# Moving accumulations and masking products on the vector engine inside a state-space loop

## The reference

```python
proj = hidden @ in_proj_w.T
gate, xBC, dt = split(proj)                  # gate and x: 8192 channels, B and C: 8 groups of 128
xBC = silu(causal_conv4(xBC))
scores = einsum(C, B) * exp(segment sums)    # Lmat, lower triangle, chunks of 128 positions
Ydiag = scores @ (x * dt)                    # within a chunk
Yoff  = C @ (carried state) * exp(cs)        # from the chunk before
y = (Ydiag + Yoff + x * D) * silu(gate)
out = y * rsqrt(mean(y*y over a group)) * norm_w @ out_proj_w.T
```

## Time and profile before

| | us |
|---|---|
| median of 3 runs | 2202.49 |
| lowest and highest | 2200.89, 2202.69 |
| the profiled execution | 2201.61 |
| span of its trace | 2199.8 |
| PE busy | 2129.0 (97%) |
| DVE busy | 1642.6 (75%) |
| ACT busy | 1431.4 (65%) |
| POOL busy | 1038.7 (47%) |

### The profile page before, as it was taken

The page is one execution under the profiler, slowest core; times in us unless marked ns, Lnnn a source line. Parts: engine busy times, 40 slices in busy tenths (PEclk is TensorE's granted clock), DMA queues, the critical chain, the costliest instruction groups (busy, mean ns, idle before and its releaser), DMA issues.

```text
span 2199.8 us, 34805 instructions
## 1 busy us (share of the span) xinstructions
PE 2129.0 (97%) x12594; PEld 1744.9 (79%) x12604; DVE 1642.6 (75%) x2661; ACT 1431.4 (65%) x3090; POOL 1038.7 (47%) x755
## 2 busy tenths in 40 slices
PE   7989989999899999999999999999999999999999
PEld 7866687887788878888888887887887888777887
DVE  7777673234888898888898888889889888886221
ACT  4388734334977677668767867767867777773332
POOL 5477544352255346344455434534445443553442
PEclk9999999999999999999999999999999999999999
DMA  3000012331423232233223323323322332231332
GB/s 134 1 1 2 1 44 83 95 92 48 168 96 135 87 125 97 87 135 126 95 87 125 130 75 113 118 78 121 135 87 87 134 135 87 87 114 49 91 96 82
DMA packets 65337, 202.53 MB, mean 92 GB/s; under 512 B 7056, under 2 KB 9104, under 8 KB 56976
## 3 DMA queue, kind: packets, MB, share of 16 engines
q1 hardware_dynamic: 65168, 200.31, 27.0%
HBM read 197.39 MB, written 2.88 MB: 91 GB/s over the span
## 4 chain that ended last, share of the span: by engine, by line
PE 83%; ACT 7%; DVE 6%; issue 3%; DMA 0%; POOL 0%; DVEq 0%; ACTq 0%; SPq 0%; POOLq 0%
PE ps L1683 78%; ACT eb L899 2%; PE ps L1987 2%; PE ps L1805 2%; PE ps L1698 1%; DVE PT L1305 1%; ACT eb L906 1%; DVE nm L1283 1%; ACT yTh L913 1%; ACT work L862 0%; DVE eb L1432 0%; ACT wAh L691 0%; ACT xc L878 0%; ACT pr_a L772 0%; DVE bst L1125 0%
## 5 line engine op out<-in xcount | busy, mean ns | idle before, releaser
L551 POOL TENSOR_TENSOR wAl<-rawA,wAh 128x512 fp32r<-128x512 f32 x233 | 339.6, 1470 | 382.5 <-ACT wAh L691 381.7
L1683 PE MATMUL ps<-xTh,wAh 128*128 128x512 f32 x1512 | 424.5, 402 | 5.7 <-DVE oacc L1500 2.6
L1683 PE MATMUL ps<-xTh,wAl 128*128 128x512 f32 x1512 | 414.7, 395 | 0.0
L1683 PE MATMUL ps<-xTl,wAh 128*128 128x512 f32 x1512 | 414.6, 395 | 0.0
L1393 DVE SCALAR_TENSOR_TENSOR work<-ps,chp,work 128x510 f32<-128x510 f32 (+2 forms) x465 | 343.9, 743 | 32.1 <-ACT work L862 22.1
L1683 PEld LDWEIGHTS ps<-xTh,wAl 128*128 128x128 f32 x1512 | 284.2, 188 | 69.4
L1683 PEld LDWEIGHTS ps<-xTl,wAh 128*128 128x128 f32 x1512 | 284.0, 188 | 69.3
L1683 PEld LDWEIGHTS ps<-xTh,wAh 128*128 128x128 f32 x1512 | 275.5, 188 | 74.9 <-issue 14.3
L557 POOL TENSOR_TENSOR wBl<-rawB,wBh 128x512 fp32r<-128x512 f32 x108 | 138.4, 1295 | 392.1 <-ACT wBh L695 392.1
L899 ACT ACTIVATE eb<-eb,gc 128x128 f32<-128x128 f32 x1008 | 307.6, 391 | 0.0
L862 ACT ACTIVATE work<-ps,gpar 128x512 f32<-128x512 f32 x155 | 119.4, 770 | 154.4 <-PE ps L1683 121.9
(11 more groups left out here) (208 smaller groups left out, 3976.7 us busy)
## 6 DMA issues: line engine op xcount, KB each, us to landing
eb<-scr_decays SPq DMA_DIRECT2D x62, 1536.0 KB, 6.5
rawA<-ma_in SPq DMA_DIRECT2D x144, 256.0 KB, 6.8
rawA<-fa_in SPq DMA_DIRECT2D x88, 256.0 KB, 2.6
rawB<-mb_in SPq DMA_DIRECT2D x64, 256.0 KB, 2.8
rawB<-fb_in SPq DMA_DIRECT2D x44, 256.0 KB, 2.6
x<-x_in SPq DMA_DIRECT2D x8, 256.0 KB, 6.0
x_out<-x SPq DMA_DIRECT2D x8, 256.0 KB, 2.7
wqraw<-wqkv_in SPq DMA_DIRECT2D x1, 1536.0 KB, 10.8
```

Of the source, the lines that this page charges most:

```text
L551: nc.gpsimd.tensor_tensor(wAl[:, slot, :], rawA[:, slot, :], wAh[:, slot, :].bitcast(F32), ALU.subtract).then_inc(A_lo, 1)
L1683: return nc.tensor.matmul(o, l, r, start=start, stop=end, **kw)
```

## The change

In odd steps the evacuation of sum 0 moves from behind both `scale_x` to between them. In steps with v = 1 and g > 0 (seven of them) both `decay_off` move from the front of the sequence to behind the evacuations, directly ahead of `decay`. Nothing else moves, and no instruction is added or taken away.

```diff
             vn = next_step(v, g)
-            if not ending and not (first and v == 0):
+            late_off = (first and v == 0) or (v == 1 and g > 0)
+            if not ending and not late_off:
                 decay_off(*vn, 0)
                 decay_off(*vn, 1)
             if not ending:
                 scale_x(*vn, 0)
+            if v % 2 == 1:
+                evacuate(v, g, 0)
+            if not ending:
                 scale_x(*vn, 1)
             if v % 2 == 1:
-                for t in range(4):
+                for t in range(1, 4):
                     evacuate(v, g, t)
-            if first and v == 0:
+            if not ending and late_off:
                 decay_off(*vn, 0)
                 decay_off(*vn, 1)
```

## The result

| | us |
|---|---|
| after, median of 6 runs | 2186.65 (2185.47 to 2188.23) |
| before, median of 6 runs | 2202.24 (2200.89 to 2202.69) |
| ratio | 0.9931, 95% interval 0.9921 to 0.9941 |
| profiled execution after | 2186.76 |
| its span | 2184.9, before 2199.8 |

The change makes the kernel 0.7% faster.

The account below looks back on a forecast made before the run. PE was taken as the bound, busy 97% of the span. Per group, -1.88 us at sum 3 became +0.4 through POOL turns, +2.8 over seven; other terms zero. Forecast median 2205.3 us, range 2188 to 2209.

Parts of the forecast that it names:

- Copy of sum 0, and `decay_off` out of its way: Step v = 1, g > 0: PE's wait ahead of sum 3 goes, -1.88 us a group, bound 13.2 in all.
- What is late next: Late `decay_off` and `decay` alternate with POOL's squares; PE waits 2.18 us for sum 7: +0.4 a group, +2.8 in all.
- the first rival: DVE has the first turn against `sqt`, or one turn is skipped: -4.4 us, 2198.1 us; chance 0.18.
- Who has the first turn: `sqt`, issued 0.13 us ahead of `decay_off`, holds the ports first by the skill page's rule; otherwise 2198.1 us.
- DVE keeps its turn over instructions in a row: Rival: only the first `decay_off` waits for `sqt`, all of the 13.2 us gain stays, 2189.3 us; chance 0.16.
- Copy of sum 0 in the first group: Step v = 1 of g = 0: no updates ahead of the copies and no wait listed, so zero.
- The additions of sum 0 in steps 3, 5 and 7: They come 0.93 us earlier, PE did not wait; the second `scale_x`, 0.60 later, is hidden by DVE's wait: zero.
- everything else: Later DVE copies in v = 2, readers of `decay_off`, and SP's and ACT's waits: no further cost or gain.

Follow-up runs that it names:

- e1: Changed kernel with both `decay_off` put back at the front, copy of sum 0 still between the two `scale_x`; measured 2194.55 us, ratio 0.9967.
- e2: Changed kernel with all evacuations behind both `scale_x` again, `decay_off` still late; measured 2204.27 us, ratio 1.0012.
- e3: Changed kernel, DVE also waits for the end of its own copy 3 ahead of the first `decay_off`; measured 2211.06 us, ratio 1.0042.
- e10: Changed kernel with two added waits: DVE for its first `update`, POOL for its own `lo_B` ahead of the squares; measured 2197.41 us (one run).
- e5: Changed kernel, DVE also waits for the end of its own copy 0 in the seven steps; measured 2210.34 us (one run).
- e8: Changed kernel with DVE's wait for its own copy 3, POOL's four squares left out in the seven steps; measured 2186.49 us, ratio 0.9928.
- e7: Changed kernel, DVE also waits for the end of its first `update` in the seven steps; measured 2211.30 us (one run).

## Why the prediction was wrong

- *Copy of sum 0, and `decay_off` out of its way*: right. The bound was 1.88 a group and 13.2 in all; measured 1.92 and 13.5. e1 and e2 show that both edits are needed for it.
- *What is late next*: this is the step that failed, in its sentence "They take turns, one instruction each" and in "Now the four POOL instructions meet four of DVE". They did not take turns. `sqt` took 4.49 in place of 1.04, both `decay_off` 1.29 in place of the 3.1 to 788.11, and the second `decay` ended at some 788.7 in place of 792.31. The +2.8 is −13.5 in truth. I had taken the turns for a fixed trait of `sqt` and `sq` meeting DVE. Two things that the sum leaned on went otherwise, the lead and the stop.
- *The lead*: `sqt` at 784.89 against `decay_off` at 785.02 is 0.13, and 0.01 to 0.04 was measured. The sum let copy 3 start 1.70 behind sum 3, as before, but 0.10 of that belonged to PE's slow start, which goes away with the wait; from the first `update` to `decay_off` it is 6.23 and not the 6.30 of the sum. With a lead of 0.13 the turns come as forecast (e3), and at 0.12 without any recent stop (e1); so a tenth of a microsecond lay between the forecast and the result.
- *The stop*: with DVE first, turns were still possible, as in e10 and in the first rival; that they did not come goes with the distance from DVE's last stop; why it does stays open. In the rows with turns that I read for this place, DVE had stood still shortly before: copy 3 for 0.55 in the earlier trace rows, the addition for 0.63 in the earlier trace rows, and the `yTl` directly ahead of the `decay_off` at 804.95 for 0.69. The change takes away that very stand-still, because PE brings sum 3 earlier: copy 3 starts without one, at 784.61, some 0.06 after it could have had sum 3 (an estimate: 782.95 and the 1.60 that is left of 1.70). The prediction's own sum has this stand-still shrink from 0.55 to 0.05 (784.37 to 784.42) and does not remark on it. e1 loses it as well and keeps its turns, because there `sq` is 0.12 ahead: taking away the stand-still was not enough by itself. The question "whom does the edit make stop waiting" was asked for PE and not for DVE.
- The arithmetic of turns was right where turns happen: e3 has 14.3 us of waits where "about 15" was forecast, and +0.41 a group where +0.4 was, in the three groups in which the clock holds; e10 has 7.1 and 2197.41 where the first rival, with one turn less, said 2198.1.
- *Who has the first turn*: the Trainium skill's page "SBUF — State Buffer", section "Who interferes with whom", has whoever issues first hold the ports for the whole instruction. Here `sqt` was issued first, by 0.01 to 0.04, in seven of seven groups, and did not get them. The measurement decides. At leads of 0.12 and more (e1, e3, e5 to e8) the page's rule and the traces agree on the first turn.
- *DVE keeps its turn over instructions in a row*, the rival at 2189.3, is what happened. I gave it 0.16, though its row, `lo_A` with 3.43, was the only one of a DVE that had not just stopped: DVE's last stop ahead of the first `decay` there is one of 0.03 us at 757.94, 9.4 us back, and the `decay` is the 15th instruction behind it; the last longer one, 1.30 us for PE, ends at 755.78. It too was a little off: its sum lets the first `decay_off` wait for `sqt`, and in fact not even that one waits. Its wait would have been hidden, so the time is not touched by it.
- *Copy of sum 0 in the first group*: taken as zero, measured 0.39. PE, before, in g = 0:

```profile
602.28 0.61 PE L1683 MATMUL ps<-wBh,yTl 128*128 128x512 f32 x2
603.00 0.73 PE L1683 MATMUL ps<-wBh,yTh 128*128 128x512 f32 x2
```

After:

```profile
602.92 0.62 PE L1687 MATMUL ps<-wBh,yTl 128*128 128x512 f32 x2
603.37 0.62 PE L1687 MATMUL ps<-wBh,yTh 128*128 128x512 f32 x2
```

The distance is 0.72 before and 0.45 after: sum 3 was 0.27 late in group 0 too, with a slower start of 0.11 behind it. The list of waits does not have so short a one, and I took its silence for a zero.

- *The additions of sum 0 in steps 3, 5 and 7*, and *everything else*: zero was right, to 0.03 us a place.
- The 1.4 at the end and the 0.61 ahead of the loop are none of the change's; without them the span would be 14.1 shorter.

## What to carry to other kernels

When a change takes a wait away, follow it on every engine: another engine may stop waiting too, and here that moved a vector instruction by a tenth of a microsecond against one of POOL's and turned an alternation into a lock-out. Before rows of a meeting of two engines are carried to a new place, look at two things, and take rows that are alike in both: which instruction is issued first and by how much, and how long before it the vector engine last stopped. If the margin is of the order of 0.1 us, the forecast has two outcomes and should carry both. A semaphore wait that an engine passes in hundredths is not free where it shifts the engine against another that shares its memory.

## What the runs showed that was not expected

- DVE goes through four instructions while a `sqt` issued 0.03 us ahead of them waits 4.49 us (alone 1.04); `lo_A` behind two `decay` was the only hint before.
- A DVE wait for its own last instruction, which leaves it idle for 0.035 us and puts the next one off by 0.115, costs 24 us of 2187 over seven groups (e3, 2211.06, against e8 without the squares, 2186.49), and does so from 11 instructions ahead (e7, 2211.30). How much of this is the stop and how much the lead of 0.13 that it gives `sqt` is not told apart; e1 has turns with such a lead alone.
- With DVE first by the same lead, the distance from its last stop goes with turns (11th instruction or nearer, up to 5.6 us) or lock-out (13th and later, from 6.9 us on); instructions and time are not told apart, and no cause in the hardware is shown.
- With turns, from the end of the other's instruction, `sqt` takes 0.98, `sq` and `lo_A` 1.22, `decay_off` 0.48, `decay` 1.00.
- In four of seven groups of e3 a stand-still of PE of 2.0 us is followed by 6 us at a mean granted clock of 0.72, and these groups are 1.5 to 1.6 us longer than the other three, in which the same stand-still is followed by 1.00.
- None of the thirteen kernels beats the changed one; e8, which is level with it, leaves work out.
